# A fused attention and expert block on one core: a sign folded into a constant row, a mask applied once, a bias as one-row products, a copy on another engine, and 34 work units in another place

## What is computed

```
x = x + tanh(g_xattn[0]) * L0_xattn(ctx, layernorm(x), mask, ...)   # 4 heads of 64
x = x + tanh(g_ffn[0])   * L0_ffn(layernorm(x), ...)                # 64 experts, grouped routing
x = x + tanh(g_xattn[1]) * L1_xattn(layernorm(x), ctx, ...)         # 16 heads of 64
x = x + tanh(g_ffn[1])   * L1_ffn(layernorm(x), ...)                # fake-quantised gated FFN

# L0_xattn: keys and values are the 1024 tokens and the 77 context tokens, queries the tokens
qn = rmsnorm(q, qn_g) * SCALE;  kn = rmsnorm(k, kn_g)
attn = where(full_mask, qn @ kn.T, -max);  attn = softmax(attn)
out = (attn @ v) @ Wo.T + bo

# L0_ffn: softmax scores, sorted per expert, 64-token groups, the best 1024 groups kept
h = silu(x @ Wup + bup) * (x @ Wgate + bgate) * share;  out = h @ Wdown + share @ bdown
```

## Time and profile before

| what | value |
|---|---|
| median of 3 runs | 2535.75 us (2531.93 to 2536.8) |
| the profiled execution, device time | 2537.17 us |
| its span, first to last instruction | 2535.3 us |
| mean granted TensorE clock | 0.893 of 2.4 GHz |
| PE busy | 2086.0 us (82%) |
| DVE busy | 1741.8 us (69%) |
| ACT busy | 1219.4 us (48%) |
| POOL busy | 664.6 us (26%) |

### The profile page before, as it was taken

How to read it: one execution, slowest core, us unless ns; L and a number is a source line. 1 busy time by engine, 2 the same in 40 slices (tenths; PEclk the granted TensorE clock), 3 DMA queues, 4 the chain that set the end, 5 groups by cost and what they waited for, 6 DMA issues and landing times.

```text
span 2535.3 us, 39154 instructions
## 1 busy us (share of the span) xinstructions
PE 2086.0 (82%) x14869; PEld 1266.5 (50%) x14874; DVE 1741.8 (69%) x2847; ACT 1219.4 (48%) x2904; POOL 664.6 (26%) x537
## 2 busy tenths in 40 slices
PE   6687778778766479579999999999999677888566
PEld 2333545546444334234566666666666445566323
DVE  3557686776879899963377667767677555565677
ACT  1355767758554266335333333333333365676346
POOL 0334867657556362000000000000000023233003
PEclk6778889898877689889999999999999898999776
DMA  4221000000000076334755455445454510000001
GB/s 141 71 70 36 2 1 2 2 1 3 1 1 1 1 258 249 135 125 188 232 156 158 145 156 155 152 154 154 157 153 156 176 36 1 1 1 1 0 1 66
DMA packets 125241, 221.91 MB, mean 88 GB/s; under 512 B 16843, under 2 KB 61887, under 8 KB 124927
## 3 DMA queue, kind: packets, MB, share of 16 engines
q1 hardware_dynamic: 109952, 168.45, 22.0%
q10 hardware_dynamic: 15103, 50.97, 5.0%
HBM read 152.63 MB, written 65.67 MB: 86 GB/s over the span
## 4 chain that ended last, share of the span: by engine, by line
PE 51%; DVE 32%; ACT 11%; issue 4%; DMA 2%; SPq 0%; POOL 0%; DVEq 0%; ACTq 0%
PE ps L436 47%; DVE arena L948 15%; DVE arena L957 7%; ACT arena L1881 6%; DVE arena L951 4%; PE ps L444 3%; DVE arena L954 3%; ACT arena L1631 2%; DVE arena L964 1%; DVE arena L960 1%; ACT arena L1891 0%; DMA arena<-share_scratch 0%; SPq L2065 0%; ACT arena L1733 0%; DMA arena<-in_clip_down 0%
## 5 line engine op out<-in xcount | busy, mean ns | idle before, releaser
L436 PE MATMUL ps<-arena 128*128 128x256 f16 (+7 forms) x13639 | 1924.9, 302 | 257.6 <-DVE arena L957 74.6
L436 PEld LDWEIGHTS ps<-arena 128*128 128x128 f16 (+3 forms) x13644 | 1113.7, 103 | 1014.5 <-issue 214.8
L948 DVE TENSOR_TENSOR arena<-arena 128x512 f32<-128x512 f32 (+6 forms) x985 | 751.1, 791 | 163.1 <-ACT arena L1836 110.9
L1631 ACT ACTIVATE arena<-ps,arena 128x512 f32<-128x512 f32 (+2 forms) x480 | 324.5, 687 | 293.9 <-PE ps L436 213.2
L1939 POOL TENSOR_TENSOR arena<-arena 128x4 f32<-128x4 f32 (+3 forms) x50 | 85.5, 1709 | 1187.6 <-DVE arena L951 1187.6
L1996 POOL TENSOR_TENSOR arena<-arena 128x512 f16<-128x512 f32 (+1 forms) x288 | 351.4, 1239 | 122.7 <-ACT arena L1631 121.4
L1836 ACT CAST arena<-arena 128x512 f16<-128x512 f32 x256 | 158.2, 618 | 458.9 <-DVE arena L948 458.9
L954 DVE SCALAR_TENSOR_TENSOR arena<-ps,arena 128x512 f32<-128x512 f32 (+4 forms) x317 | 219.9, 698 | 218.5 <-PE ps L436 181.0
L444 PE MATMUL ps<-arena 128*128 128x128 f32 (+2 forms) x1230 | 205.0, 310 | 185.8 <-DVE arena L951 98.0
L948 DVE TENSOR_TENSOR arena<-ps,arena 128x512 f16<-128x512 f32 (+10 forms) x427 | 222.0, 553 | 185.7 <-ACT arena L1635 47.5
L1631 ACT ACTIVATE arena<-ps 128x512 f16<-128x512 f32 (+1 forms) x512 | 274.2, 609 | 77.9 <-PE ps L436 74.6
(11 more groups left out here) (74 smaller groups left out, 479.8 us busy)
## 6 DMA issues: line engine op xcount, KB each, us to landing
arena<-share_scratch SPq DMA_DIRECT2D x512, 128.0 KB, 3.0
wide_scratch<-arena ACTq DMA_DIRECT2D x96, 512.0 KB, 2.6
arena<-wide_scratch SPq DMA_DIRECT2D x96, 512.0 KB, 4.5
mq_scratch<-arena SPq DMA_DIRECT2D x16, 308.0 KB
vw_scratch<-arena SPq DMA_DIRECT2D x32, 154.0 KB
arena<-mq_scratch SPq DMA_DIRECT2D x16, 308.0 KB, 5.3
arena<-vw_scratch SPq DMA_DIRECT2D x8, 576.0 KB, 6.4
arena<-in_x SPq DMA_DIRECT2D x4, 1024.0 KB, 11.3
```

The source lines that it names most:

```text
L436: return e.matmul(o, l, r, start=start, stop=stop, skip_group_check=True)
L948: return e.tensor_tensor(o, a, b, op)
L1631: return e.activation(o, i, f, bias=bias, scale=scale)
```

## The change

Six things are done.

1. The constant row 64 of the keys (`KB`, `KBc`) is -1 and no longer +1, so the maximum itself goes into row 64 of `QB`: NEG is one instruction and no longer two.
2. The context keys are multiplied by the mask once for each batch, in place in `KAc`, at set-up (C5); KM is one instruction for each head where it was a mask product and a combination. The mask tiles `mb` and `mn` become float16.
3. The copy `QB[0:64]` from `QA` leaves VectorE's KM. ScalarE writes it in TR straight from the PSUM bank, with the same scale, as a second activation behind that of `QA`, for each head and half of the queries (32 in all, of 64x512). The bank is free when this one ("qc") and VectorE's low half ("ql") are done.
4. The bias bo is no longer spread over 128 partitions, scaled by the gate and added to x by VectorE (16 additions of 128x512). It stays one row, split in float16 high and low, and PB adds it in PSUM by products of a row of ones with these rows (64 products of 256 columns, one partition deep). Its load is one row.
5. VectorE's waits on "x1" count one for each PB where they counted two.
6. In HOIST, 58 half units stand between turn 2 and the first count where 24 stood; 13 are left behind the last turn where 47 were.

```
-    mu, mb, mn = L.take([308], U8), L.take([308]), L.take([308])
+    bo_, boh, bol, one16 = L.take([256]), L.take([256], F16), L.take([256], F16), L.take([128], F16)
+    mu, mb, mn = L.take([308], U8), L.take([308], F16), L.take([308], F16)
...
-    for steps_, then in ([(80, [("turn", 2)]), (24, [])] + ...
+    for steps_, then in ([(80, [("turn", 2)]), (58, [])] + ...
...
-            empty[bk] = [("qa" if w else "ka", 4 * g + h + 1), ("ql" if w else "kb", 4 * g + h + 1)]
+            empty[bk] = [("qc" if w else "ka", 4 * g + h + 1), ("ql" if w else "kb", 4 * g + h + 1)]
...
-                    m = mm3(bank(7)[:, 256 * t:256 * t + 256], ..., k == 0, k == 1)
+                    mm3(bank(7)[:, 256 * t:256 * t + 256], ..., k == 0, False)
+                mm(bank(7)[:, 256 * t:256 * t + 256], one16[0:1], boh[0:1], False, False)
+                m = mm(bank(7)[:, 256 * t:256 * t + 256], one16[0:1], bol[0:1], False, True)
...
-            ts(boB, boB, gat[:, 4:5], None, ALU.mult)
+            cp(boh[0:1], bo_[0:1])
+            e.memset(one16[0:1], 1.0)
+            tt(bol[0:1], bo_[0:1], boh[0:1], ALU.subtract)
...
+            W.wait_ge("ctl", 2 + b + 1)
+            tt(KAc[:, b], KAc[:, b], rep(mb[...], [128, 4, 77]), ALU.mult).then_inc(S["cmask"], 1)
...
-                e.memset(KB[64:65], 1.0)
+                e.memset(KB[64:65], -1.0)
...
-            W.after(W.own(tt(KM[:, h, :], KAc[:, b, h, :], mb[:, 77 * b:77 * b + 77], ALU.mult)))
-            stt(KM[:, h, :], mn[...], KA[:, h, 0:1], KM[:, h, :], ALU.mult,
+            stt(KM[:, h, :], mn[...], KA[:, h, 0:1], KAc[:, b, h, :], ALU.mult,
                 ALU.add).then_inc(S["km"], 1)
-            W.wait_ge("qa", 8 * b + 5 + h)
-            cp(QB[0:64, h, :], QA[0:64, h, :]).then_inc(S["qc"], 1)
...
-            W.after(W.own(tt(MX[:, h, :], MX[:, h, :], MC[:, h, :], ALU.max)))
-            ts(MN[:, h, :], MX[:, h, :], -1.0, None, ALU.mult).then_inc(S["mn"], 1)
+            tt(MN[:, h, :], MX[:, h, :], MC[:, h, :], ALU.max).then_inc(S["mn"], 1)
...
-            W.wait_ge("x1", 4 * g + 2 * j + 1)
-            tt(y, y, rep(boB.unsqueeze(1), [128, 2, 256]), ALU.add).then_inc(S["x1"], 1)
...
                 e.activation(QA[:, h, c0:c0 + 512], bank(bk), ACT.Copy, scale=g2).then_inc(S["qa"], 1)
+                e.activation(QB[0:64, h, c0:c0 + 512], bank(bk)[0:64], ACT.Copy, scale=g2[0:64]).then_inc(S["qc"], 1)
```

More of the change, by code:

```diff
@@ L128, in emit @@
     g2, kg = L.take([1]), L.take([1])
-    boB = L.take([256])
-    mu, mb, mn = L.take([308], U8), L.take([308]), L.take([308])
+    bo_, boh, bol, one16 = L.take([256]), L.take([256], F16), L.take([256], F16), L.take([128], F16)
+    mu, mb, mn = L.take([308], U8), L.take([308], F16), L.take([308], F16)
     mcu, mc = L.take([4], U8), L.take([4])
@@ L359, in early_until @@
         return [(("up", "gate")[i % 2], i // 2) for i in range(at, n)]
-    for steps_, then in ([(80, [("turn", 2)]), (24, [])] + [(0 if i == 0 else 2, [("count", i)]) for i in range(11)]
+    for steps_, then in ([(80, [("turn", 2)]), (58, [])] + [(0 if i == 0 else 2, [("count", i)]) for i in range(11)]
                          + [(2, [("rank",)]), (7, [("above",)]), (3, [("tied",)]), (5, [("shares", 0), ("shares", 1)])]
@@ L600, in SCO @@
             W.wait_ge("kb", 8 * b + 5 + h)
-            W.wait_ge("qc", 4 * b + h + 1)
+            W.wait_ge("qc", 8 * b + 5 + h)
             W.wait_ge("qm", 4 * b + h + 1)
@@ L646, in PB @@
                 for k in range(2):
-                    m = mm3(bank(7)[:, 256 * t:256 * t + 256], (OTh[:, 2 * t + k, :], OTl[:, 2 * t + k, :]),
-                            (WOh[:, k, :], WOl[:, k, :]), k == 0, k == 1)
+                    mm3(bank(7)[:, 256 * t:256 * t + 256], (OTh[:, 2 * t + k, :], OTl[:, 2 * t + k, :]),
+                        (WOh[:, k, :], WOl[:, k, :]), k == 0, False)
+                mm(bank(7)[:, 256 * t:256 * t + 256], one16[0:1], boh[0:1], False, False)
+                m = mm(bank(7)[:, 256 * t:256 * t + 256], one16[0:1], bol[0:1], False, True)
             m.then_inc(S["py"], 1)
-            empty[7] = [("x1", 4 * g + 2 * j + 1)]
+            empty[7] = [("x1", 2 * g + j + 1)]
         def RT(g, k):
@@ L1035, in C1 @@
             m.then_inc(S["wsplit"], 1)
-            e.memset(KBc[64:65], 1.0)
+            e.memset(KBc[64:65], -1.0)
             e.memset(VCh[:, :, :, 64], 1.0)
@@ L1076, in C5 @@
                ALU.subtract).then_inc(S["ctl"], 1)
+            W.wait_ge("ctl", 2 + b + 1)
+            tt(KAc[:, b], KAc[:, b], rep(mb[:, 77 * b:77 * b + 77].unsqueeze(1), [128, 4, 77]), ALU.mult).then_inc(S["cmask"], 1)
         def PU(i):
@@ L1163, in KMT @@
             W.wait_ge("mx", 36 * (b - 1) + 9 * h + 3)
-            W.wait_ge("cact", 10)
-            W.after(W.own(tt(KM[:, h, :], KAc[:, b, h, :], mb[:, 77 * b:77 * b + 77], ALU.mult)))
+            W.wait_ge("cmask", b + 1)
             W.wait_ge("ka", 8 * b + h + 1)
-            stt(KM[:, h, :], mn[:, 77 * b:77 * b + 77], KA[:, h, 0:1], KM[:, h, :], ALU.mult,
+            stt(KM[:, h, :], mn[:, 77 * b:77 * b + 77], KA[:, h, 0:1], KAc[:, b, h, :], ALU.mult,
                 ALU.add).then_inc(S["km"], 1)
-            W.wait_ge("qa", 8 * b + 5 + h)
-            cp(QB[0:64, h, :], QA[0:64, h, :]).then_inc(S["qc"], 1)
         def MXT_(b, h, j):
@@ L1220, in RA @@
         def RA(g):
-            W.wait_ge("x1", 4 * g + 4)
+            W.wait_ge("x1", 2 * g + 2)
             stats(g)
@@ L2073, in sync @@
         load("wB", WO, I["WoT"].rearrange("(k p) n -> p k n", p=128))
-        load("wB", boB, I["bo0"].partition_broadcast(128))
+        load("wB", bo_[0:1], I["bo0"].unsqueeze(0))
         load("wB", mu, I["mask"].rearrange("b j -> (b j)").partition_broadcast(128))
```

## The result

The changed kernel takes 2461.82 us (median of 4, 2452.33 to 2464.06) beside 2533.84 for the kernel before: a ratio of 0.9708, 95% interval 0.9679 to 0.9738, which is 74 us less (66 to 81). I had forecast 48 less, 2488 us, and a range down to 2467. The direction and the main term were right; the gain is half as large again as forecast, and lies outside the range.

A forecast was written before the change was run, and what follows sets the result against it. VectorE sets the end up to 1092 us, TensorE behind it, and no engine is full in the first attention. The sum -44 - 16 + 11 + 0 + 1 = -48 from 2535.75 gives 2488 us, range 2467 to 2501.

The forecast's parts named there:

- the main term: Largest term of the sum: 34 half units moved into TensorE's idle time ahead of the first count, -44 us.
- The 34 half units: Ahead of the first count: moved units fill TensorE's gap and shorten its work behind, -44 us (-41 to -45).
- the lateness at the count: At the first count: TensorE ends at 1095.2, 2.3 us behind the 1092.85 at which it takes the count now.
- VectorE's three small instructions a head: First attention: copies, negations and mask products, 26.0 us busy, leave VectorE; 0.6 of it counts, -16 us (bounds 0 and 26).
- the first rival: First attention: the small instructions count in full, and TensorE's clock may rise; -66 us, 2470 us; chance 0.20.
- a fifth of these stretches: First attention, VectorE at 80%: the rest is VectorE waiting for TensorE, so only 0.6 of the saving was taken.
- The stretch: First attention, batch 2: VectorE busy 82.19 of 103 us among the maxima, little more than half of the turning stretch.
- The copy on ScalarE: Turning stretch: 32 more activations of 0.57 us cost ScalarE 18 us, 0.6 of it shows, +11 us (bounds 0 and 18).
- The bias: VectorE loses 12 us of additions, TensorE gains 11 to 15 us of products; they nearly cancel, 0 (-12 to +15).
- The set-up: Set-up: four products of the context keys with the mask cost 1.8 us on VectorE; taken as +1 us (0 to +2).
- The second, that the waits inside them stay: First attention: other instructions inherit the removed ones' waits, only short times go; -39 us, 2497, up to 2503; chance 0.17.

The follow-up runs named there:

- hoist_only: The kernel before with only the 34 half units moved ahead of the first count: 2493.27 us, ratio 0.9845.
- small_only: The kernel before with only the sign in the constant row and the context masked once: 2503.82 us, ratio 0.9891.
- dose_psum: The changed kernel with one more small VectorE instruction a head, reading PSUM, ahead of the last maximum, result unread: 2470.75 us, ratio 0.9746.
- dose_behind: The changed kernel with one more small VectorE instruction a head, out of SBUF, directly behind the one that ends NEG: 2469.41 us, ratio 0.9752.
- dose_sbuf: The changed kernel with one more small VectorE instruction a head, out of SBUF, ahead of the last maximum, result unread: 2472.19 us, ratio 0.9755.
- dose_turn: The changed kernel with 16 more small VectorE instructions out of SBUF, behind the keys' low halves in the turning stretch: 2458.56 us, ratio 0.9708.
- copy_both: The changed kernel with ScalarE writing the query copy and VectorE writing it once more in KM: 2470.98 us, ratio 0.9759.
- after_copy_back: The changed kernel with the query copy back on VectorE in KM: 2459.15 us, ratio 0.9714.
- copy_only: The kernel before with only the query copy moved to ScalarE: 2532.52 us, ratio 1.0002.
- bias_only: The kernel before with only the bias as one-row products, and the mask tiles in float16: 2536.82 us, ratio 1.0014.

## Why the prediction was wrong

**The 34 half units: right.** Forecast -44 (-41 to -45). Measured -39 alone (34 to 45 by the interval; 43.5 by the profiled spans) and -44 in company. The clock of 1.00 behind the count and the steady pace came out as read, and TensorE's part behind the count is 46 us shorter for 44. The step on the lateness at the count was wrong though its size was met: I had TensorE 2.3 us late, and VectorE was, by 2.8 in hoist_only, 1.8 of it at the swap. That the two sizes agree is luck.

**VectorE's three small instructions a head: the step that failed.** The prediction said "Bounds: 0 if TensorE sets the end there, 26 if VectorE does throughout", and took 0.6 of it, -16. The runs give 13 us for the negations, 13 for the mask products and 13 for the copies, some 40 where busy time said 26. With them the sum is -44 - 40 + 11 + 0 + 1 = -72, beside the 74 measured. Not only the share was too low; the upper bound was no bound. I had bounded the gain by the busy time of what was removed. That this fails is firmest without the copies: small_only gains 28 us (23 to 32) for 15.5 of busy time. It shows two things beside it: VectorE's other instructions took less time as well (26.5 us less where 15.5 were removed), and TensorE ran the same products in 17 us less, at a granted clock of 0.90 for 0.87. I had named the second in the first rival ("less waiting may also raise it") and given it no number. The reason for my 0.6, that a fifth of these stretches is VectorE waiting for TensorE, was no measure of what comes back, and it was too high: of the 103 us of the earlier trace rows VectorE waits 13.8 for TensorE and 6.3 for ScalarE. Added instructions show the same from the other side: in dose_psum 2.5 us of bare time cost 10.

**The stretch: right.** VectorE's time counts among the maxima (dose_behind, dose_sbuf) and has room in the turning stretch (dose_turn), as the busy times of 82.19 of 103 and 24.27 of 45 us had it.

**The copy on ScalarE: right, within a wide interval.** Forecast +11, measured +11 (copy_both against after_copy_back), 4 to 18; that the numbers are equal is luck. With the 13 of VectorE's copy the edit as a whole is nothing (copy_only, -2 to 3 us); I had it at 5 more.

**The bias: right in size.** Forecast 0; measured 0 to 7 more alone, nothing in company. The one-row products take as long as full ones: the stretch of bias_only has records of 48 of them, 9.3 us busy, with a mean of 274 ns beside 272 for the products of 128 rows and 256 columns. That VectorE's 12 us and TensorE's 11 to 15 cancel is still argued: no run has the one without the other, and both could be hidden.

**The set-up.** No run has its +1 alone, and it can't be seen: the stretch above starts 3.0 us earlier in small_only than before, and 2.6 us earlier in copy_only, which leaves the set-up as it was.

**The rivals.** The first, that the small instructions count in full, is the one nearest to what happened, at 2470; even that was 8 us short. The second, that the waits inside them stay, fell: the negation went with all of its 0.52 us and more. What is true of it is that the long cases are waits, and that a wait moves: adding a neighbour changed the next instruction by 350 ns (dose_psum).

The trace of the kernel before shows what they wait for. While the long copy of the earlier trace rows runs, from 333.34 to 334.72, GpSimd has this:

```profile
333.19 1.25 POOL L1996 TENSOR_TENSOR arena<-arena 128x512 f16<-128x512 f32 x1 [0.20 <-ACT arena L1631]
```

It starts ahead of the copy and ends at 334.44, and the copy ends 0.28 us behind it. At the short copy, 467.18 to 467.59, GpSimd is at rest. It is so with all 48 copies, negations and mask products of that trace. 17 start while a TENSOR_TENSOR of GpSimd runs; they take 0.44 to 1.39 us, and each ends 0.03 to 0.28 us behind that one. The other 31 take 0.17 to 0.42 us. The 128 maxima over 1024 keys, reductions out of PSUM, take 1.19 to 1.23 us whether GpSimd runs at their start (74) or not (54). By the Trainium skill (SBUF — State Buffer, "Who interferes with whom") VectorE and GpSimd exclude each other at a shared pair of ports, for the whole of an instruction, where VectorE's has two inputs in SBUF or runs in a two-port mode, and a reduction takes no part. The trace agrees, in these 48 and 128 cases; in the stretch of the attention GpSimd is busy for 362 of 579 us. So the busy time of the removed instructions held waits for GpSimd, and so did that of their neighbours.

**Left open.** In small_only the stretch's 27.8 us are 17 of TensorE's busy time, which go with its clock, and 11 of its idle time. Which of these the shorter waits on VectorE cause, and whether the clock would have risen without them, can't be told from these runs: both moved together in each of them. No run here took GpSimd's work away, so how many of the 40 us its turns make up is open too.

## What to carry to other kernels

The busy time of removed instructions was no upper bound for what they brought, where two engines wait for each other in turn: price one with a run that adds or removes a few of the same size in the same stretch, here 0.6 to 0.8 us for an instruction of 0.15 to 0.5 us, and nothing in the stretch next to it. An instruction whose duration has two values, here 0.41 and 1.38 us for one shape, holds a wait: look on the other engines' timelines for what ends just ahead of it. Work that moved from one of these engines to another bought nothing here (the copy: 13 against 11; the bias: 0), work that went away did. And the gap on the engine that is the bound behind it could be filled from behind at its full length; once it was filled, moving eight more units was neither gain nor loss.

## What the hardware showed unexpectedly

TensorE's 4695 products of the attention took 458.5 us before and 441.3 us with 32 small instructions of VectorE less, at a granted clock of 0.87 and 0.90. VectorE's unchanged query copy of 64x1024 took 656 ns in the mean before, 411 with the same change. Its long cases start while a TENSOR_TENSOR of GpSimd runs and end 0.28 us behind it, while reductions out of PSUM take 1.19 to 1.23 us with or without one. A swap of two 512 KB transfers kept VectorE waiting 4.4 us in the runs without the move, and 5.4 to 6.5 us in those with it.
